# SyncE's order of chunk stores and loads, moved one tile sooner in a fused attention and mixture-of-experts kernel

## The reference, cut to what matters

```python
x = x + cross_attention(layernorm(x), ctx)   # scores against 77 context rows and the row's own key, softmax, values
h2 = layernorm(x)
qkv = h2 @ W_qkv + b_qkv                      # 16 heads of 32, self attention over 512 rows
gate = softmax(h2 @ W_gate + b_gate); top_g, top_i = top_k(gate, 2)     # 8 experts
moe = sum over the two experts e of top_g * (h2 @ W_experts[e] + b_experts[e])
out = x + self_attention(qkv) + moe
```

## Time and profile before

| | before |
|---|---|
| median of three runs | 1504.75 us |
| profiled execution | 1504.87 us, span 1503.2 us |
| PE busy | 1344.3 us (89%) |
| PE weight load busy | 991.1 us (66%) |
| DVE busy | 951.8 us (63%) |
| ACT busy | 905.6 us (60%) |
| POOL busy | 358.7 us (24%) |
| chain that ended last, by engine | PE 34%, ACT 16%, DVE 15%, DMA 15%, issue 12% |

### The profile page before, as it was taken

How to read it: one execution, slowest core, us unless ns; L and a number is a source line. 1 busy time by engine, 2 the same in 40 slices (tenths; PEclk the granted TensorE clock), 3 DMA queues, 4 the chain that set the end, 5 groups by cost and what they waited for, 6 DMA issues and landing times.

```text
span 1503.2 us, 25227 instructions
## 1 busy us (share of the span) xinstructions
PE 1344.3 (89%) x6720; PEld 991.1 (66%) x6721; DVE 951.8 (63%) x2047; ACT 905.6 (60%) x1856; POOL 358.7 (24%) x572
## 2 busy tenths in 40 slices
PE   4988888889898889999999999999999878999997
PEld 4957777777776556665666665666665346777775
DVE  4246656666666897777777777777777633334332
ACT  4123333333334888998999999999999843333332
POOL 0001112121111001121111212102001007777765
PEclk9999899988889999999999999999999779999998
DMA  5014555555557433745435473454647867877874
GB/s 153 1 65 153 196 196 187 203 186 201 183 184 225 139 78 94 154 99 135 90 103 133 98 182 77 85 138 105 154 98 177 285 225 127 142 133 131 142 136 57
DMA packets 111368, 212.44 MB, mean 141 GB/s; under 512 B 28265, under 2 KB 36585, under 8 KB 109139
## 3 DMA queue, kind: packets, MB, share of 16 engines
q1 hardware_dynamic: 82048, 166.13, 37.1%
q0 software_dynamic: 26624, 42.04, 16.7%
q10 hardware_dynamic: 2643, 3.65, 0.8%
HBM read 79.48 MB, written 77.73 MB: 105 GB/s over the span
## 4 chain that ended last, share of the span: by engine, by line
PE 34%; ACT 16%; DVE 15%; DMA 15%; issue 12%; SPq 3%; POOL 3%; ACTq 1%; POOLq 0%; DVEq 0%
DMA plain<-in_L_ffn_W_experts_dram 9%; PE banks L1077 8%; PE banks L221 6%; ACT banks L762 6%; PE banks L223 6%; PE banks L222 6%; DVE plain L1532 6%; ACT plain L772 5%; PE banks L1061 3%; DVE parts L1546 3%; DMA plain<-h_rows,score_bias 3%; PE banks L1041 2%; DMA out_dram<-plain,score_bias 2%; ACT plain L656 2%; DVE st L1226 1%
## 5 line engine op out<-in xcount | busy, mean ns | idle before, releaser
L221 PE MATMUL banks<-parts 128*128 128x512 f32 (+6 forms) x1108 | 449.4, 406 | 54.7 <-DVE parts L1239 22.2
L223 PE MATMUL banks<-parts 128*128 128x512 f32 (+6 forms) x1108 | 430.1, 388 | 0.0
L222 PE MATMUL banks<-parts 128*128 128x512 f32 (+6 forms) x1108 | 429.7, 388 | 0.0
L762 ACT ACTIVATE banks<-banks,plain 128x512 f32<-128x512 f32 x512 | 340.4, 666 | 54.3 <-DVE plain L1532 53.0
L1532 DVE TENSOR_REDUCE plain<-banks 128x1 f32<-128x512 f32 x512 | 329.1, 685 | 64.0 <-PE banks L1041 60.9
L221 PEld LDWEIGHTS banks<-parts 128*128 128x128 f32 (+1 forms) x1108 | 219.5, 198 | 106.6 <-issue 43.3
L772 ACT ACTIVATE plain<-banks 128x1024 f32<-128x1024 f32 x256 | 263.7, 1030 | 32.0 <-PE banks L1061 28.7
L223 PEld LDWEIGHTS banks<-parts 128*128 128x128 f32 (+1 forms) x1108 | 218.8, 197 | 40.8
L222 PEld LDWEIGHTS banks<-parts 128*128 128x128 f32 (+1 forms) x1108 | 220.2, 199 | 32.0
L1041 PE MATMUL banks<-parts 96*128 96x512 f32 x512 | 197.1, 432 | 3.1 <-ACT banks L762 2.7
L1061 PE MATMUL banks<-parts 104*128 104x512 f32 x512 | 173.7, 421 | 11.1 <-ACT plain L772 10.3
(11 more groups left out here) (180 smaller groups left out, 1510.0 us busy)
## 6 DMA issues: line engine op xcount, KB each, us to landing
parts<-parts SPq DMA_DIRECT2D x384, 128.0 KB, 2.7
experts_split<-parts SPq DMA_DIRECT2D x32, 512.0 KB, 4.2
h_turned<-parts SPq DMA_DIRECT2D x32, 512.0 KB, 2.9
parts<-h_turned SPq DMA_DIRECT2D x32, 512.0 KB, 6.7
parts<-experts_split SPq DMA_DIRECT2D x8, 2048.0 KB, 10.6
plain<-in_x_dram SPq DMA_DIRECT2D x32, 256.0 KB, 4.2
plain<-in_L_ffn_W_experts_dram SPq DMA_DIRECT2D x32, 256.0 KB, 4.3
out_dram<-plain SPq DMA_DIRECT2D x32, 256.0 KB, 3.1
```

Of the source, the lines that this page charges most:

```text
L221: pe.matmul(out, stat[0], mov[0], start=first, stop=False)
L222: pe.matmul(out, stat[0], mov[1], start=False, stop=False)
L223: return pe.matmul(out, stat[1], mov[0], start=False, stop=last)
L762: act.activation(bank[SB[t]][:], bank[SB[t]][:], ACT.Exp, bias=nmx[:, k, t:t + 1], accum_out=Z[:, t, k:k + 1]).then_inc(q["f_exp"], 1)
```

## The change

SyncE's work on tile i begins with the store of chunk i (and so with the wait for `ws_lo` of chunk i), and the load of chunk i+2 follows it. Before, it began with the store of chunk i-1 and the load of chunk i+1. The store of the last chunk, which came after the loop, is now inside it. Nothing else is changed: the same transfers, the same buffers, the same work on the other engines.

```diff
             def tiles(b, more, first=False):
                 for t in range(T):
-                    if t or not first:
-                        store_chunk(b + (t - 1) // T, (t - 1) % T)
-                    if t and (more or t < T - 1):
-                        load_chunk(b + (t + 1) // T, (t + 1) % T)
-                    elif not first and t == 0:
-                        load_chunk(b, 1)
+                    store_chunk(b, t)
+                    if more or t < T - 2:
+                        load_chunk(b + (t + 2) // T, (t + 2) % T)
                     if not more and t == 2:
 
                         sp.wait_ge(q["v_full"], NT)
...
             tiles(B - 1, False)
-            store_chunk(NE - 1, C - 1)
             turned_out(NT - 1, T - 1)
```

## The result

The changed kernel takes 1429.64 us (median of four, 1425.94 to 1435.01) against 1506.15 us for the kernel before beside it (four, 1502.65 to 1510.84): a ratio of 0.9493, 95% interval 0.9451 to 0.9535. Forecast were 1435 us and 1427 to 1460. The profiled execution took 1431.03 us, its span 1429.4 us, 73.8 less than before.

What follows compares the result with a forecast made beforehand. The prediction took a closed loop through the W_experts chunk load as the bound, 10.79 us a step; 74.7 - 3.0 - 1.5 = 70.2 us gained, from 1504.87 to 1435 us, range 1427 to 1460 (8 in 10).

Steps and rivals of the forecast that it cites:

- The loop through the load: Tile steps: chunk load issued only after `h2_norm(i-1)`, next ScalarE step waits for it; 10.79 us a step, 4.3 leaving the loop.
- The new wait for `ws_lo` at nothing: SyncE, before storing chunk i: `chunk_lo(i)` ends at about the same time as `h2_norm(i-1)`, so the wait costs nothing.
- No hand-offs: Rival, tile steps: the two loops collide, each step keeps a 0.5 us wait, 8.8 us a step, 1450 us; chance 0.17.
- TensorE's 8.23 us a step, taken as 8.3: Tile steps: TensorE's work without gaps, 7.96 mean plus at most 0.27 for `p_turn`; 30 x (10.79 - 8.3) = 74.7 us gained.
- The second loop, 7.90: Tile steps: the loop over VectorE, ScalarE and GpSimd without the load sums to 7.90 us, less than TensorE's 8.23.
- The clock: TensorE in the tile steps: nearly full clock expected; rival: it stays at 0.88, 9.35 us a step, 1466 us; chance 0.09.
- x: Load of x before `h_stats`: 6.7 us of room against 4.2; rival: 0.7 us late, 20 us lost, 1455 us, chance 0.04.
- The split weights, 3.0 us: Behind the last batch's first step, ScalarE and VectorE split weights; charged 3.0 us lost (0 to 3.7).
- The stage's end, 1.5 us: N0, TensorE's first self-attention product, waits for SyncE's fetch of the turned tiles; 1.5 us lost (0 to 3).
- what comes after N0 is as before: Everything behind N0, TensorE's first product of the self attention, was to take as long as before: no gain or loss.

Runs made afterwards that it cites:

- load_only: The kernel before, with SyncE loading chunk i+2 in its work on tile i but still storing chunk i-1 there; 1488.57 us.
- value_one: The changed kernel with two of the three matmuls in `value` left out, so its values are less exact; 1419.06 us.
- value_first: The changed kernel with `value(31)` moved up right behind `score(31)` in TensorE's last step; 1427.82 us.
- tuned: The changed kernel with `value(31)` moved up behind `score(31)` and the weights' splitting moved to where ScalarE and VectorE wait; 1422.56 us.
- traffic2: The changed kernel with two more transfers of 512 KB a tile ahead of x's load; 1460.79 us.

## Why the prediction was right

Step by step, by its own terms:

- **The loop through the load.** Right: who waits for the load fell from 186.7 us to the first chunk's 7.1, and the landing didn't change. That the store came late beside the load was read from its issue and landing times alone; load_only shows it.
- **The new wait for `ws_lo` at nothing.** Right: VectorE's `chunk_lo`, which raises `ws_lo`, is through at 246.88, before SyncE so much as issues the turned tile, at 247.81.

```profile
246.18 0.70 DVE L1293 TENSOR_TENSOR parts<-plain,parts 128x512 fp32r<-128x512 f32 x1
...
247.81 0.33 SPq L347 DMA_DIRECT2D h_turned<-parts  x1
248.75 0.56 SPq L358 DMA_DIRECT2D experts_split<-parts  x1
```

  From that issue to the chunk's store SyncE takes 0.52, 0.94, 0.58 and 0.69 us in turn, from start to start. In the kernel before it was 0.52, 0.96, 0.52 and 0.63, so this alternation isn't the new wait.
- **No hand-offs.** Right: in the 30 steps TensorE's matmuls wait three times, 1.5 us in all, where that rival had 0.5 us in every step.
- **TensorE's 8.23 us a step, taken as 8.3.** Right in mechanism, 0.2 to 0.3 too long. The 7.96 for all but `p_turn` hold; `p_turn` takes only 0.11 us before the next matmul can go (the chain after counts "0.11 PE banks L942"), not its duration of 0.27: 8.07, the mean of 7.95 and 8.19. The 0.07 added for collisions were nothing. Without the 1.4 us of the split weights, which the forecast has in a term of its own, the mean of all 30 steps is 8.03: 8.0 us less than 30 x 8.3.
- **The second loop, 7.90.** It measures 7.62 in value_one; in the changed kernel it doesn't bind.
- **The clock.** Expected near 1.00, was 1.00, from 0.88. The Trainium skill's rule on transposes ("TensorE: Matmul & The Clock Gate", Part 4: PE-mode transpose) gave the rival with the clock its chance; with 9 transposes in each step, and four tiny matmuls in every second, nothing was lost, so this trace doesn't bear that rival out.
- **x.** Landing 4.1 us at a DMA share of 0.72, against 4.2 before: no rise. The Trainium skill ("DMA: Bandwidth & Descriptors", Latency and other measured facts) gives 0.2 us for an access on average and 2 us at high load, which the prediction took as a rise of 1.8; these runs show 1.4 more at a share of 0.95 and 2.3 at 0.99, with extra bytes in front.
- **The split weights, 3.0 us.** 1.4 measured (1.05 and 0.39 above the usual steps), in the range of 0 to 3.7, but half of what was charged. value_one, where the second loop has no spare, pays 3.2: so the spare hides more than I took it to.
- **The stage's end, 1.5 us.** 1.51, and N0 waits for the fetch, as forecast. Not foreseen was what this wait of 5.5 us does to the clock. N0 runs at half clock, 1.2 GHz, from 378.39 to about 383.5; in the kernel before, where the clock had fallen at a wait of 3.3 us, only from 459.24 to 461.0. These 3.4 us more at half speed are the 1.59 in the ledger, against "what comes after N0 is as before".

The forecast was 70.2 us of gain. The traces show 81.3 + 1.1 - 1.5 - 1.6 = 79.3 up to the first scores, and 73.8 with the scatter behind it; the medians 76.5. In the 30 steps alone 71.7 were forecast (74.7 - 3.0) and 81.3 came, 9.6 more: 8.0 from the length of the step, 1.6 from the weights. That the two traces differ by only 3.6 us from the forecast is partly luck, since the scatter of 5.4 and the half clock of 1.6 took most of it back.

## What to carry to other kernels

Where a transfer's wait is on the chain in every step, ask for its loop: what must be over before it is issued, and what can't begin before it has landed. Moving the request one step sooner hides it whole when the room (a step less the issuing queue's delay) exceeds the landing. Look for the transfer that lands second, since a wait for two names only the later: here either move alone brought under a third of the gain that both brought together. The new bound is the sum of starts, not of durations, of the next engine; and what waits nowhere before, such as the fetch at the stage's end, can become late when the stage before it has no gaps left.

## What the runs showed of the hardware

- A gap costs twice when the clock falls in it. After 5.5 us of waiting TensorE did N0's matmuls with a granted clock of 0.50 until about 383.5, 0.43 us apart instead of 0.23. With a gap of 3.3 us further ahead the half-clock time fell mostly on the little work before N0: N0 was at full clock from its start in value_first, and from 377.3, 1.0 us after its start, in tuned.
- With the waits gone the granted clock of the stage is 1.00 instead of 0.88, and TensorE's busy time for the same matmuls fell by a seventh (281.7 to 241.1 us). But the wait of about 1.2 us before `score` in every step was mostly not enough to bring the clock down. value_one has it 28 times (29.1 us in all), and between 160 and 340 us TensorE, busy 85% of the time, kept the full clock:

```profile
160.00:340.00 180.00, 153.41 (x990) 129.15 (x988) 160.29 (x476) 88.57 (x201) 49.31 (x188) 1.00 0.78 272
```

  In the kernel before, a second wait, before L946, stands shortly ahead of it. The clock fell ten times in the 30 steps, nine times soon after such a pair (0.7 to 2.7 us and 1.1 to 1.2) and once after a single wait of 1.9 us. It also fell once in value_one (at 128.9 us) and once in traffic2 (at 154.1) with under 0.3 us of waiting ahead of the 1.2; what decides was not tested.
- Copies from device memory to device memory beside the rest filled the DMA engines (share 0.99) at 343 GB/s, where a short stretch without them moves more (after, 377 to 379 us: share 1.05 at 411 GB/s). That the copies are the cause was not tested apart.
